# Correcting clipped states in the mixer: whole sequences against stretches of 256 steps

## The reference, cut to what matters

```python
A = -jnp.clip(jnp.exp(A_log), -10.0, -0.01)     # 0.01 everywhere, as exp is above zero
def step(h, x_t):
    h = jnp.clip(h * A[None] + x_t[:, :, None] * Bm[None], -10.0, 10.0)
    y = jnp.einsum('bid,id->bi', h, C)
    return (h, y)
...
out_f = _ssm_scan(x_ssm, A, B_mat, C_mat, reverse=False)
out_b = _ssm_scan(x_ssm, A, B_mat, C_mat, reverse=True)
out = (out_f + out_b) * 0.5 * jax.nn.silu(gate)
return jnp.einsum('bli,di->bld', out, out_proj_w)
```

## Time and profile before

| | us |
|---|---|
| median of 3 runs | 3650.48 (3649.37 to 3654.43) |
| the profiled execution | 3632.42 |
| its span, first to last instruction | 3630.7 |
| first stage, to the start of the next | about 621 |

### The profile page before, as it was taken

How to read it: one execution, slowest core, us unless ns; L and a number is a source line. 1 busy time by engine, 2 the same in 40 slices (tenths; PEclk the granted TensorE clock), 3 DMA queues, 4 the chain that set the end, 5 groups by cost and what they waited for, 6 DMA issues and landing times. The chain is left out here.

```text
span 3630.7 us, 31977 instructions
## 1 busy us (share of the span) xinstructions
PE 2780.5 (77%) x10138; PEld 1386.8 (38%) x10146; DVE 2030.0 (56%) x3662; ACT 1358.6 (37%) x1980; POOL 927.1 (26%) x608
## 2 busy tenths in 40 slices
PE   2007888999999979999877776882999998377317
PEld 1003434555555534444344452351333332155303
DVE  7997541222222266666454449213777776678587
ACT  1004433211111146666543320341777777233003
POOL 0003565000000000000122220303899999000005
PEclk6558999999999989999978879996999999688558
DMA  2002112000000065445300020112000000100000
GB/s 52 0 0 47 47 47 64 0 0 0 0 0 0 0 138 145 145 138 146 97 1 0 1 72 0 51 46 71 1 1 1 9 1 1 32 1 1 2 0 29
DMA packets 107447, 125.99 MB, mean 35 GB/s; under 512 B 22283, under 2 KB 60300, under 8 KB 107052
## 3 DMA queue, kind: packets, MB, share of 16 engines
q1 hardware_dynamic: 105260, 120.13, 12.4%
q0 software_dynamic: 2048, 4.20, 0.4%
HBM read 108.55 MB, written 14.16 MB: 34 GB/s over the span
## 5 line engine op out<-in xcount | busy, mean ns | idle before, releaser
L2360 PE MATMUL dots_x<-all_xt,delta_wE 128*128 128x512 f32 x768 | 364.0, 610 | 3.6 <-DVE dots_g L2455 2.2
L2345 POOL TENSOR_TENSOR dots_pr<-dots_g 128x512 f32<-128x512 f32 (+2 forms) x96 | 305.6, 3204 | 63.4 <-DVE dots_g L2455 55.5
L1012 DVE SCALAR_TENSOR_TENSOR attn_sim<-attn_sc,attn_mask 128x512 f32<-128x512 f32 (+3 forms) x256 | 125.8, 492 | 316.9 <-PE attn_sc L938 313.8
L949 PE MATMUL attn_op<-attn_sim,attn_v 128*128 128x512 f32 (+3 forms) x768 | 295.0, 486 | 0.0
L938 PE MATMUL attn_sc<-attn_q,attn_xb 128*128 128x512 f32 (+3 forms) x768 | 295.0, 486 | 0.0
L1298 DVE TENSOR_TENSOR grp_h<-grp_sq,grp_cb 128x512 f32<-128x512 f32 x256 | 176.5, 692 | 191.9 <-ACT grp_sq L1186 171.7
L1126 PE MATMUL grp_po<-grp_h,grp_down 128*128 128x512 f32 x512 | 266.4, 602 | 5.7 <-DVE grp_h L1298 5.6
L1118 PE MATMUL grp_ph<-all_xt,grp_up 128*128 128x512 f32 x512 | 264.0, 598 | 0.5 <-ACT grp_sg L1202 0.5
L2452 DVE TENSOR_TENSOR dots_m<-dots_x,dots_sg 128x512 f32<-128x512 f32 x256 | 173.9, 689 | 148.3 <-PE dots_x L2360 142.1
L1180 ACT ACTIVATE grp_r<-grp_ph 128x512 f32<-128x512 f32 x272 | 162.5, 597 | 185.2 <-PE grp_ph L1118 183.6
L2360 PEld LDWEIGHTS dots_x<-all_xt,delta_wE 128*128 128x128 f32 x768 | 135.1, 189 | 233.2 <-issue 138.6
(11 more groups left out here) (614 smaller groups left out, 4933.8 us busy)
## 6 DMA issues: line engine op xcount, KB each, us to landing
grp_cb<-grp_combine SPq DMA_DIRECT2D x512, 128.0 KB, 3.1
mix_cb<-top_weights SPq DMA_DIRECT2D x64, 256.0 KB, 3.2
cap_xs<-cap_zero SPq DMA_DIRECT2D x7, 320.0 KB, 4.6
experts_xe<-cap_xs SPq DMA_DIRECT2D x7, 320.0 KB, 3.2
all_x<-in_L_attn_x_dram SPq DMA_DIRECT2D x4, 512.0 KB, 5.0
cap_w<-in_L_ffn_W_dram SPq DMA_DIRECT2D x1, 2048.0 KB
cap_ys<-experts_yo SPq DMA_DIRECT2D x8, 256.0 KB, 2.3
delta_h<-all_xn SPq DMA_DIRECT2D x1, 2048.0 KB
```

The source lines that it names most:

```text
L949: ins = nc.tensor.matmul(op[half][:, n0 - half * GROUP:n0 - half * GROUP + w], v[:, par, m], sim[:, par, k, 0:w], start=False, stop=False)
L2345: nc.gpsimd.tensor_tensor(slot[w % SLOTS][:, at:at + n], a_, b_, ALU.mult).then_inc(pool_ready, 1)
L2360: nc.tensor.matmul(bank(n, sh)[:], wE[:, 1 - k % 2, a, sh], XTj[:, k // 2, par::2], start=True, stop=True).then_inc(u_mm, 1)
```

## The change

The sequence of each row is cut into 4 stretches of 256 steps. Maxima, flags and words are kept for each of the 16 pairs of row and stretch, and a second word for each row has one bit for each of its 4 stretches. The loop over the rows loads that second word first, tests the stretches one by one, and only within a stretch that has a bit loads its word and tests groups and dimensions as before. A correction works on 288 steps, the 256 of its stretch and 32 before them, and adds 256 to G. S gets 32 zeros ahead of each row. The first instruction of a correction signals no longer, and each batch has a semaphore of its own. The two weight matrices that were loaded into q are now loaded into y.

```diff
--- before.py
+++ after.py
@@ -237,6 +237,10 @@
     TPB = SEQ // P
...
     HB, RB, CB = 5, 3, 6
+    LEAD, CHUNK = 32, 256
+    NCHUNK = SEQ // CHUNK
+    NCELL = NSEG * NCHUNK
+    WINDOW, ROW = LEAD + CHUNK, LEAD + SEQ
...
@@ -264,20 +268,25 @@
         gain = s.sb("gain", [P, CT])
         decay = s.sb("decay", [P, 1])
         limS, nCBS = (s.sb(n, [P, NSEG, DS]) for n in ("limS", "nCBS"))
-        d0 = s.sb("d0", [P, SEQ, 2])
-        d1 = s.sb("d1", [P, SEQ, 2])
-        q = s.sb("q", [P, SEQ, 2])
-        wi = q[:, 0:2 * CT * C // 2].rearrange("p (k c) a -> p k (c a)", k=2 * CT)
-        wo = q[:, SEQ // 2:SEQ // 2 + DI // 2].rearrange("p c a -> p (c a)")
+        d0 = s.sb("d0", [P, WINDOW, 2])
+        d1 = s.sb("d1", [P, WINDOW, 2])
+        q = s.sb("q", [P, WINDOW, 2])
         xs, gate, y = (s.sb(n, [P, CT, SEQ]) for n in ("xs", "gate", "y"))
-        S, G = (s.sb(n, [P, NSEG, SEQ]) for n in ("S", "G"))
-        mx = s.sb("mx", [P, NSEG, 1])
-        reach = s.sb("reach", [P, NSEG, DS])
-        most = s.sb("most", [P, NSEG * DS])
-        bit = s.sb("bit", [1, NSEG, DS])
-        flags = s.sb("flags", [1, NSEG, DS])
-        mask_f = s.sb("mask_f", [1, NSEG])
-        masks = s.sb("masks", [1, NSEG], mybir.dt.int32)
+        wi = y[:, 0, 0:2 * CT * C].rearrange("p (k c) -> p k c", k=2 * CT)
+        wo = y[:, 1, 0:DI]
+        S = s.sb("S", [P, NSEG, ROW])
+        G = s.sb("G", [P, NSEG, SEQ])
+        S_flat, G_flat = S[:].rearrange("p k t -> p (k t)"), G[:].rearrange("p k t -> p (k t)")
+        mx = s.sb("mx", [P, NSEG, NCHUNK])
+        reach = s.sb("reach", [P, NSEG, NCHUNK, DS])
+        most = s.sb("most", [P, NCELL * DS])
+        bit = s.sb("bit", [1, NCELL, DS])
+        flags = s.sb("flags", [1, NCELL, DS])
+        mask_f = s.sb("mask_f", [1, NCELL])
+        masks = s.sb("masks", [1, NCELL], mybir.dt.int32)
+        cell_f = s.sb("cell_f", [1, NSEG, NCHUNK])
+        cell_sum = s.sb("cell_sum", [1, NSEG])
+        cell_masks = s.sb("cell_masks", [1, NSEG], mybir.dt.int32)
...
@@ -302,8 +311,9 @@
...
-        reach_ready, most_ready, out_mm, x_added, ch, fix, apart = (s.sem(n) for n in (
-            "reach_ready", "most_ready", "out_mm", "x_added", "vector_chain", "fix", "apart"))
+        reach_ready, most_ready, out_mm, x_added, ch, apart = (s.sem(n) for n in (
+            "reach_ready", "most_ready", "out_mm", "x_added", "vector_chain", "apart"))
+        fix = [s.sem(f"fix{b}") for b in range(BATCH)]
...
@@ -633,7 +643,7 @@
                 def largest(b):
                     pool.wait_ge(reach_ready, b + 1)
                     pool.sem_inc(apart, 1)
-                    nc.gpsimd.partition_all_reduce(most[:], reach[:].rearrange("p s d -> p (s d)"), P, bass.bass_isa.ReduceOp.max).then_inc(most_ready, 1)
+                    nc.gpsimd.partition_all_reduce(most[:], reach[:].rearrange("p s c d -> p (s c d)"), P, bass.bass_isa.ReduceOp.max).then_inc(most_ready, 1)
 
                 largest(0)
                 largest(1)
@@ -654,45 +664,48 @@
                 c = Chain(dve, ch)
                 tt, ts, stt, redu = nc.vector.tensor_tensor, nc.vector.tensor_scalar, nc.vector.scalar_tensor_tensor, nc.vector.tensor_reduce
 
-                def correct(b, k, d):
-
+                def correct(b, k, c_, d):
                     n = k * DS + d
-                    done = (b * (NSEG * DS) + n) * 4
-                    sk = S[:, bass.ds(k, 1), :].rearrange("p a t -> p (a t)")
-                    gk = G[:, bass.ds(k, 1), :].rearrange("p a t -> p (a t)")
+                    done = ((k * NCHUNK + c_) * DS + d) * 3
+                    sk = S_flat[:, bass.ds(k * ROW + c_ * CHUNK, WINDOW)]
+                    gk = G_flat[:, bass.ds((k * NCHUNK + c_) * CHUNK, CHUNK)]
                     L = limS[:].rearrange("p k d -> p (k d)")[:, bass.ds(n, 1)]
                     w = nCBS[:].rearrange("p k d -> p (k d)")[:, bass.ds(n, 1)]
-                    ts(d1[:, :, 0], sk, -1.0, L, ALU.mult, ALU.add).then_inc(fix, 1)
-                    ts(d1[:, :, 1], sk, L, None, ALU.add).then_inc(fix, 1)
-                    dve.wait_ge(fix, done + 2)
+                    ts(d1[:, :, 0], sk, -1.0, L, ALU.mult, ALU.add)
+                    ts(d1[:, :, 1], sk, L, None, ALU.add).then_inc(fix[b], 1)
+                    dve.wait_ge(fix[b], done + 1)
                     nc.vector.tensor_tensor_scan(q[:].rearrange("p t a -> p (t a)"), d0[:].rearrange("p t a -> p (t a)"),
-                                                 d1[:].rearrange("p t a -> p (t a)"), 0.0, ALU.mult, ALU.min).then_inc(fix, 1)
-                    dve.wait_ge(fix, done + 3)
-                    stt(gk, q[:, :, 1], w, gk, ALU.mult, ALU.add).then_inc(fix, 1)
+                                                 d1[:].rearrange("p t a -> p (t a)"), 0.0, ALU.mult, ALU.min).then_inc(fix[b], 1)
+                    dve.wait_ge(fix[b], done + 2)
+                    stt(gk, q[:, LEAD:, 1], w, gk, ALU.mult, ALU.add).then_inc(fix[b], 1)
 
                 def scan(b, k):
                     if k % CT == 0:
                         dve.wait_ge(pj_used, 8 * b + 4)
                     dr, ct = divmod(k, CT)
                     src = xs[:, ct] if dr == 0 else xs[:, ct, ::-1]
-                    c.link(nc.vector.tensor_tensor_scan(S[:, k], decay[:].to_broadcast([P, SEQ]), src, 0.0, ALU.mult, ALU.add))
+                    c.link(nc.vector.tensor_tensor_scan(S[:, k, LEAD:], decay[:].to_broadcast([P, SEQ]), src, 0.0, ALU.mult, ALU.add))
 
                 def reaches(b):
                     dve.sem_inc(scanned, 1)
-                    c.link(redu(mx[:], S[:], AX.X, ALU.max, apply_absolute_value=True))
+                    c.link(redu(mx[:], S[:, :, LEAD:].rearrange("p k (c t) -> p k c t", t=CHUNK), AX.X, ALU.max, apply_absolute_value=True))
                     for dr in range(2):
-                        last = tt(reach[:, dr * CT:(dr + 1) * CT], absB[:], mx[:, dr * CT:(dr + 1) * CT].to_broadcast([P, CT, DS]), ALU.mult)
+                        last = tt(reach[:, dr * CT:(dr + 1) * CT], absB[:].unsqueeze(2).to_broadcast([P, CT, NCHUNK, DS]),
+                                  mx[:, dr * CT:(dr + 1) * CT].unsqueeze(3).to_broadcast([P, CT, NCHUNK, DS]), ALU.mult)
                     last.then_inc(reach_ready, 1)
 
                 def gains(b):
                     for k in range(NSEG):
-                        c.link(ts(G[:, k], S[:, k], gain[:, k % CT:k % CT + 1], None, ALU.mult))
+                        c.link(ts(G[:, k], S[:, k, LEAD:], gain[:, k % CT:k % CT + 1], None, ALU.mult))
 
                 def take_masks(b):
                     dve.wait_ge(most_ready, b + 1)
                     c.link(stt(flags[:], most[0:1].rearrange("p (s d) -> p s d", d=DS), BOUND * 0.999, bit[:], ALU.is_gt, ALU.mult))
                     c.link(redu(mask_f[:], flags[:], AX.X, ALU.add))
                     c.link(nc.vector.tensor_copy(masks[:], mask_f[:]))
+                    c.link(stt(cell_f[:], mask_f[:].rearrange("p (k c) -> p k c", c=NCHUNK), 0.5, bit[:, 0:NSEG, 0:NCHUNK], ALU.is_gt, ALU.mult))
+                    c.link(redu(cell_sum[:], cell_f[:], AX.X, ALU.add))
+                    c.link(nc.vector.tensor_copy(cell_masks[:], cell_sum[:]))
 
                 def statistics_in(b):
                     dve.wait_ge(x_in[b], 16)
@@ -717,22 +730,29 @@
                 def corrections(b):
                     dve.sem_inc(apart, 1)
                     with dve.Fori(0, NSEG) as k:
-                        mask = dve.value_load(masks[0:1, bass.ds(k, 1)], min_val=0, max_val=2 ** DS - 1)
-                        for quad in range(DS // QUAD):
-                            with dve.If((mask & (((1 << QUAD) - 1) << (quad * QUAD))) > 0):
-                                for d in range(quad * QUAD, (quad + 1) * QUAD):
-                                    with dve.If((mask & (1 << d)) > 0):
-                                        correct(b, k, d)
+                        cells = dve.value_load(cell_masks[0:1, bass.ds(k, 1)], min_val=0, max_val=2 ** NCHUNK - 1)
+                        for c_ in range(NCHUNK):
+                            with dve.If((cells & (1 << c_)) > 0):
+                                mask = dve.value_load(masks[0:1, bass.ds(k * NCHUNK + c_, 1)], min_val=0, max_val=2 ** DS - 1)
+                                for quad in range(DS // QUAD):
+                                    with dve.If((mask & (((1 << QUAD) - 1) << (quad * QUAD))) > 0):
+                                        for d in range(quad * QUAD, (quad + 1) * QUAD):
+                                            with dve.If((mask & (1 << d)) > 0):
+                                                correct(b, k, c_, d)
+                                            with dve.Else():
+                                                dve.sem_inc(fix[b], 3)
+
+                                        dve.sem_inc(apart, 1)
                                     with dve.Else():
```

(9 more changed lines are left out.)

## The result

The changed kernel takes 3728.03 us (median of 4 runs, 3725.38 to 3729.74) against 3649.93 for the kernel before (4 runs, 3648.39 to 3654.43): a ratio of 1.0211 (95% interval, here and below in brackets: [1.0194, 1.0229]), 78 us slower. The forecast was 3707, 57 slower than the median it was laid on.

The account below looks back on a forecast made before the run. DVE was taken to bound 44 to 262 us, PE 303 to 621. Batch 0 -99, its far jumps +39, PE's waits +48.3, +27.0, +31.8, clock +6, POOL +3: +56, hence 3707 us on the median; range 3550 to 3790.

Parts of the forecast that it names:

- Batch 0, corrections: DVE in batch 0: 28 corrections on 288 steps take 2.06 us each, 57.7 us in place of 168.
- Batch 0, tests: DVE in batch 0: tests, loads, correction starts and entering new code take 55.8 us, far jumps counted separately.
- Price of a far jump: Failed stretch tests and branches back on DVE: each costs 2.6 us above a near jump, bounds 0 to 5.0.
- Every pass pays: DVE's row loop: the far-jump cost recurs in every pass, 15 jumps in batch 0, 19 in each later batch.
- Who waits: PE waits for a late y in batches 1, 2 and 3, by 48.3, 27.0 and 31.8 us.
- p: Cost of one far jump on DVE above a near one, taken as 2.6 us; total change -131 + 72 p.
- Clock and POOL: After PE's waits, outputs at a fallen clock cost 6 us; POOL's wider reduction adds 3 us in batches 2 and 3.
- rival 1: Far jumps on DVE cost no more than near ones: -96 us, 3554 us; chance 0.10.
- 3 (p = 1.6): A far jump on DVE costs 1.6 us above a near one: -16 us, 3635 us; chance 0.11.
- rival 2: Only the first pass of each batch pays for far jumps: -77 us, 3574 us; chance 0.12.
- rival 4: At a far jump the neighbouring page's fetch must end first, 5 us each: +229 us, 3880 us; chance 0.10.
- rival 5: Each pair is flagged in all four stretches, giving 112 corrections in batch 0: at least 3860 us; chance 0.02.

Follow-up runs that it names:

- e4: The changed kernel testing and correcting only one fixed stretch per row, the one with the peak, without stretch tests, in a body of 255 instructions: 3553.49 us.
- e10: The kernel before plus one test that never holds, jumping over four dead groups of corrections, body 468 instructions: 3709.47 us against 3636.28 for the kernel before.
- e11: The kernel before plus one test that never holds, jumping over sixteen dead groups of corrections, body 1092 instructions: 3721.73 us against 3636.28 for the kernel before.
- e2: The row guard: the changed kernel plus one test of the whole row word, so that an empty row jumps over all its stretches at once: 3590.94 us.
- e3: The changed kernel with the tests and corrections of batches 1 to 3 left out of the program: 3594.12 us.
- e5: The changed kernel with a row-word test first, then a hardware loop over the four stretches with one stretch-word test each: 3567.76 us, ratio to before 0.9766.

## Why the prediction was right, and where not

- **Batch 0, corrections.** Forecast 28 x 2.06, measured 28 x 2.22 (+4.5 us). The scan was sized well, 1.36 against 1.33; the two writes and their handovers take 0.69 up to the scan (49.15 to 49.84) where 0.58 had stood. L680 takes 0.48, not 0.36.
- **Batch 0, tests.** 55.8 had been set for them. From the first L674 (49.15) to the last L680 (202.59) are 153.4 us, where 57.7 + 55.8 + 39 = 152.5 had been forecast. How they split, e4 shows: without stretch tests and far jumps it takes 106.2 us from first to last (48.03 to 154.23), of which 62.2 are corrections and 44.0 tests, 2.4 less than the 46.4 that the same items had. The stretch tests, second words and 15 far jumps together are the other 47.2, 1.2 less than their 9.4 + 39; what a jump alone costs in batch 0 is not shown. The 3 us for entering new code, part of the 55.8, were set by 8 pages, a count that no run shows; what the trace shows of new code there are 34 instruction packets in 44:205. Batch 0 in all: PE's first wait fell by 58.4 where the steps had -99 + 39 = -60. Small errors offset each other, which is in part luck.
- **Price of a far jump.** 2.6 was forecast, from a bracket of 0 to 5.0. It was the author's estimate and no row shows it: the stop in the rows is 1.6 us above a near test (2.0 against 0.4), and when code is asked for no run shows. Measured in its place are 3.1 between two failed stretch tests, 2.8 as the mean of a late pass, and again 3.1 from the mean idle time before y in batches 1 to 3, 67.2 us (201.7 over 3) where 55 to 65 had stood: (67.2 - 9.8 + 2) / 19, with 9.8 for that idle time before (29.3 over 3) and 2 for the stall in it. This is the term that was undersized. The row guard's lone stop is 2.8 us from branch to landing, with one packet (407.5:411). The stops of the changed kernel are 3.1 us, with two packets in the one looked at; that the second is the cause is not shown.
- **Every pass pays.** Right in the changed kernel (8.4 packets a pass on average). The reason, "because the loop is four times what the passes of before are seen to keep", holds only in part. In batches 1 to 3 the edge lies at 312 to 370 instructions, and past it not the loop's length but the places touched between two returns decide: e10 and e11, 468 and 1092 instructions long, have 135.9 and 134.6 us before y, and e2 jumps over 1042 in passes of 1.47 us. No row of before could tell this.
- **Who waits.** Forecast 48.3, 27.0 and 31.8 for the three new waits of PE; measured 62.7, 33.8 and 37.9. With p = 3.1 the same steps give 57.8, 36.5 and 41.3, in sum 135.6 for the measured 134.4: the slack was read rightly, and the error of the sum is p's. The single waits are off by -4.9, +2.7 and +3.4 and cancel, as the idle time before y was 73.1, 60.4 and 68.2 us and not the same in each batch: that the sum fits so closely is luck.
- **Clock and POOL.** 6 us for outputs at a fallen clock, measured 6.4. POOL's reduction takes 1.08 us where the earlier trace rows had 0.54 and 2.1 had been feared; e3 gives it no visible part.

The sum: waits 107.1 forecast, 134.4 measured; batch 0 -60 and -58.4; the small terms 9, and 4.4 as what is left to the +80.4 of the first stage. So nearly all of the miss of 24 us is in the three waits. Rivals 1 (p = 0) and 3 (p = 1.6) fell with the 3.5 us spacing, rival 2 (only first passes pay) with the last pass, rival 4 (p = 5) with the same rows, and rival 5 with the 28 scans. What rival 1 had put the change at, 3554, is about what e4 takes (3553), which has no far jump but leaves out three quarters of the cells; e5, which computes everything, reaches 3568.

## What to carry to other kernels

A hardware loop with tests in it was only cheap here while its passes fetched next to nothing. All loops of up to 312 instructions without a far place were of that kind (75 to 77 packets in the whole run); one of 370 was in batch 0 and not in the other three (5 packets a pass); and 253 with one far place were not (4.5 to 4.8), while the row guard's two small places, 1042 instructions apart, were (1.47 us a pass). Beyond the edge y waited 11 us a pass at 370 instructions and 16 at 718, where it had waited 3 at 312, also for code that never runs. When finer flags multiply the unrolled body, loop over them instead, and ask the coarsest word first, so that the usual case is one jump (e5, 3567.76 us against 3728.03). Batches with nothing to do pay for the tests of those that have: count them against their slack, as the three new waits of PE and not the corrections decided here.

## What the hardware showed that I had not expected

- A jump over 1042 instructions and back cost no more than a near one in the later passes of e2's batch 3 (1.47 us for a whole pass, where a near one would be 1.1 + 0.4). Only the first stops, for 2.8 us.
- The edge is sharp: one more group of 58 instructions takes y's idle time in batches 1 to 3 from 39.0 to 132.7 us. And it is not the same in every batch: in batch 0 the same loop fetched nothing after its first pass (no packet in 87:264).
- y's four instructions go with what POOL does. In the kernel before L738 took 2.17 us in the earlier trace rows, with POOL busy all through; the L737 of the same batch before it took 1.23, with PE busy all through and ACT for 0.77 us, but POOL for none (windows of before: length, then busy PE, PEld, DVE, ACT, POOL, clock, DMA):

```profile
317.27:318.50 1.23, 1.23 (x4) 0.57 (x3) 1.23 (x1) 0.77 (x2) 0.00 (x0) 1.00 1.06 157
321.99:324.16 2.17, 2.17 (x6) 0.76 (x4) 2.17 (x1) 1.14 (x2) 2.17 (x2) 1.00 0.33 121
```

  In the changed kernel POOL stands still during the late y, and all four take 1.23: 2 to 3 us came back in this way in each of batches 1 to 3. PE and ACT alone don't slow them, then. POOL is the likely cause, but not shown: an L737 at 383.90 took 1.23 as well, with POOL busy for 0.91 of it, and no run changes POOL's work alone.
